# Second group's term rows: four instead of eight transposes each, half of them summed by an accumulating DMA, and two steps moved

## Chip, core and metric

One NeuronCore of a Trainium2 chip runs the whole program. The metric is the device time of one execution in microseconds. A profiled execution has a span (first to last instruction) and a time of its own, which is a little longer than the span.

## What is computed

A block of two parts over 16 sequences of 128 channels by 256 positions. The first part multiplies two projections of a context, convolves the products with a long kernel for each head, and contracts the result with the normalised input; the second is a mixture of eight experts with a capacity, beside a shared feed-forward.

```python
kv = jnp.einsum('bhil,bhjl->bijhl', k_, v_)                  # 8 x 8 products per head, k_ = v_ = ctx
y = irfft(rfft(kv, 2L) * rfft(ssm_kernel, 2L))[..., :L]      # causal convolution of each
out = jnp.einsum('bijhl,bhil->bjhl', y + kv * D, q_)         # q_ = layernorm(x): a sum over i, eight terms
x = x + tanh(g_xattn) * out
x = x + tanh(g_ffn) * moe(layernorm(x))                      # argmax of 8 logits, capacity 256, experts + shared
```

## The kernel before

The 16 sequences are four groups of four (`NG`, `GB`), numbered 0 to 3. The convolution of a group is eight units of two heads; with four groups there are 32 units, one in each **slot** s = 0 to 31 (`CONV` = 32). All engines have the same loop over slots (TensorE at line 1357, DVE at 1124, ACT at 864, POOL at 678), each with its own part of the work, in an order that is written out by hand. The tables `STEPS`, `FIRST_STEPS`, `THIRD_STEPS` and `LAST_STEPS` say how many slots after the end of a group's convolution a step of that group stands; `due(step, s)` turns them into "which group's step is due in slot s". Engines execute in order, and semaphores carry the dependences, so a step that waits holds up everything behind it on its engine.

In a slot s < 32:

- TensorE convolves the unit (`convolve`, lines 1203 and 1206), into one of two places `z`; it must find the products of two units before done (`prods`).
- DVE multiplies the convolution by the queries (`products`, line 509) into `terms`: for each of the unit's two heads eight rows, the eight terms of the sum over i. Six instructions per unit.
- POOL prepares later groups' context products (`kv_products`, lines 490 and 493, every second slot), and for the groups from `FULL_TERMS` = 2 on it adds rows 4 to 7 to rows 0 to 3 of the unit one slot ago (`fold`, line 662).

When a group's eight units are through, TensorE turns `terms` back (`turn_r`, line 1231, two halves k = 0 and 1 in two slots): for each of four 128-column pieces it transposes the rows one after the other into the same place of PSUM, which sums them. `terms_of(g)` is 8 for groups 0 and 1 and 4 for the folded ones: 32 or 16 transposes for each half. DVE adds the result to x (`first_residual`, line 957), and takes the statistics for the second norm (`norm_stats`, lines 923 to 929); POOL makes scale and bias of them (`scale_and_bias`, lines 634 and 635), ACT normalises (`normalise`, line 739), TensorE turns the tokens (`turn_xT`), and ACT and DVE split them into high and low halves (lines 783 and 1070). Router and shared feed-forward follow on TensorE (line 1294), with a silu on ACT (806) and a multiply on DVE (1026) behind each use; the router's logits are copied by ACT (803), turned by TensorE (1255), and DVE chooses the expert (`choose`, lines 974 to 991).

The first norm of a group's queries runs ahead: statistics, scale and apply of group g at slots 8(g-1) + 1, + 2 and + 2, its turn (`turn_q`, line 1218) at 8(g-1) + 5. For group 3 that is 17, 18, 18 and 21. Statistics, scale and apply share single buffers, so the norms go through DVE, POOL and ACT one after another in the order in which their statistics stand.

The places of the change in the code: `FULL_TERMS`, `FIRST_STEPS`, `due`, the fold in POOL's loop (line 683) and the waits of `turn_r` (line 1224). Slots 13 to 21, about 44 to 71 us of the profile, are the stretch in which group 1 is convolved to its end, group 0's tokens go through the router (slots 15 and 16), group 1 is turned (slots 17 and 18) and group 2's convolution has begun (slot 16 on).

Of the kernel before, what the change touches and what calls it, by code (L numbers as in the profile page):

```python
# [32 lines left out]
ALU = mybir.AluOpType  # L33
# [8 lines left out]
NG = 4  # L42
# [17 lines left out]
UNITS = H // 2  # L60
# [11 lines left out]
REST_SLOT = 21  # L72
TERMS = 8
TURNS = 22
FULL_TERMS = 2
HEADS = 24
TROW = HEADS * 64
EXPERT_SPLIT_SLOT = CONV + 12
# [8 lines left out]
    "turn_r0": 1, "turn_r1": 2, "residual0": 2, "residual1": 3, "ln2_stats": 3, "ln2_scale": 4, "ln2_apply": 5,  # L87
    "turn_xT": 6, "tokens_low": 7, "logits": 10, "exp": 10, "places": 12, "gate": 12, "scatter": 12,
}
FIRST_STEPS = {"ln2_stats": 3, "ln2_scale": 3, "ln2_apply": 4, "turn_xT": 5, "tokens_low": 6, "logits": 9, "exp": 9}  # L90
THIRD_STEPS = {"ln2_apply": 4, "logits": 9, "exp": 9, "places": 10, "gate": 10, "scatter": 10}
OWN_STEPS = (FIRST_STEPS, {}, THIRD_STEPS)
LAST_STEPS = {
# [1 line left out]
    "turn_xT": 4, "tokens_low": 5, "logits": 7, "exp": 7, "gate": 8, "places": 9, "scatter": 9,  # L95
}
SCATTER_REST = {24: 0, CONV: 1}
PREPARING = ("ln1_stats", "ln1_scale", "ln1_apply", "turn_q")


def due(step, s):

    if step in PREPARING:
        g, late = divmod(s - STEPS[step], UNITS)
        return g + 1 if late == 0 and 0 < g + 1 < NG else -1
    if s == CONV + LAST_STEPS[step]:
        return NG - 1
    for g, own in enumerate(OWN_STEPS):
        if s == UNITS * (g + 1) + own.get(step, STEPS[step]):
            return g  # L110
    return -1
# [8 lines left out]
def unit(s):  # L120

    g, i = divmod(s, UNITS)
    return g, (i + 4 * (g % 2)) % UNITS
# [97 lines left out]
def build(nc, x, ctxt, kpad, skip_d, g_x, g_f, wg, w1, w3, w2, sw1, sw3, sw2, out):  # L221
# [4 lines left out]
    with ExitStack() as ctx:  # L226
# [3 lines left out]
        def sem(name):  # L230
            return ctx.enter_context(nc.semaphore(name))
# [126 lines left out]
        z_ready = sem("z_ready")  # L358
        prods = sem("prods")
        folded = sem("folded")  # L360
        expert_memory = sem("expert_memory")
        tp_ready = sem("tp_ready")
        tp_free_act = sem("tp_free_act")
# [24 lines left out]
        def view(t, off, dims, parts=P):  # L388

            a = t[:]  # L390
            row = a.ap[0][0]
            return bass.AP(a.tensor, a.offset + off, [[row, parts], *dims])
# [228 lines left out]
        def _(pool):  # L621
# [35 lines left out]
            def fold(s):  # L657
# [3 lines left out]
                             for i in range(2))  # L661
                pool.tensor_tensor(low, low, high, ALU.add).then_inc(folded, 1)  # L662

            def scatter(g, parts):
                for b in parts:
                    n = GB * g + b
                    pool.indirect_dma_start(  # L667
                        out=xd, out_offset=bass.IndirectOffsetOnAxis(ap=dest[:, n:n + 1], axis=0),
                        in_=xrow[:, g % 2, b, :], in_offset=None, bounds_check=E * CAP - 1,
                        oob_is_err=False).then_inc(scattered[g % 2], 16)  # L670
# [7 lines left out]
            for s in range(SLOTS):  # L678
                g, i = kv_due(s)
                if g >= 0:  # L680
                    kv_place_free(pool, g, i)
                    kv_products(pool, g, i, 1, kv_pool)
                if 1 <= s <= CONV and unit(s - 1)[0] >= FULL_TERMS:
                    fold(s - 1)
                for what in ("ln1", "ln2"):
                    if due(what + "_scale", s) >= 0 and (what, due(what + "_scale", s)) != ("ln1", 1):
                        scale_and_bias(NORM_AT[(what, due(what + "_scale", s))])
                if s == SLOTS - 1:
                    pool.wait_ge(z_ready, CONV)
                    pool.memset(bg[:, :, :, :], 0.0).then_inc(pool_consts, 1)  # L690
                g = due("scatter", s)
                if s in SCATTER_REST:
                    scatter(SCATTER_REST[s], range(2, GB))
                if g >= 0:
                    if g == 0:
                        pool.wait_ge(xd_zeroed, 16 * 4)
                    if g >= 2:
                        pool.wait_ge(scattered[g % 2], 16 * GB)
                    pool.iota(xrow[:, g % 2, :, L + 1:L + 2], pattern=[[P, GB], [1, 1]], base=1 + g * GB * P,
                              channel_multiplier=1, allow_small_or_imprecise_dtypes=True).then_inc(numbered, 1)  # L700
                    pool.wait_ge(numbered, g + 1)
                    pool.wait_ge(dest_done, g + 1)
                    pool.wait_ge(gate_done, g + 1)
                    scatter(g, range(2 if g in SCATTER_REST.values() else GB))
                if s == SPLIT_SLOT:
                    split_up()
# [476 lines left out]
        def _(pe):  # L1183
# [37 lines left out]
            def turn_r(g, k):  # L1221
                pe.wait_ge(prods, UNITS * (g + 1))
                if g >= FULL_TERMS:
                    pe.wait_ge(folded, UNITS * (g + 1 - FULL_TERMS))
                n = TP_AT[("r", g, k)]
                tp_wait(pe, n)
                for j in range(2 * BLK):
                    b, blk = 2 * k + j // BLK, j % BLK
                    for t in range(terms_of(g)):
                        src = view(terms, t * TROW + first_head(g, 0) * 64 + blk * GB + b, [[PL, CH]])  # L1230
                        mm = pe.matmul(tp[n % 2][:, j * P:(j + 1) * P], src, ident[:, :], is_transpose=True,  # L1231
                                       start=(t == 0), stop=(t == terms_of(g) - 1))
                mm.then_inc(tp_ready, 1)
# [177 lines left out]
```

## Time and profile before

| | |
|---|---|
| three runs, us | 214.48, 215.14, 214.38; median 214.48 |
| profiled execution, us | 214.29, its span 212.6 |
| mean granted TensorE clock | 0.991 |
| busy in the span | TensorE 198.7 us, DVE 159.9, POOL 123.8, ACT 91.9 |

All times in rows are us from the span's start. A row of the timeline merges equal instructions that follow each other: start, duration until the last of them ends, engine, line, operation, written and read tiles, shape, count, and in brackets how long the engine was idle before and who ended that. Instructions of one engine overlap a little, so the distance from one start to the next is what an instruction takes of its engine.

### The profile page before, as it was taken

Reading aid. Unit: us, or ns where it says so; the run is one execution under the profiler, and the core shown is the slowest. Engines: PE = TensorE matmul, PEld = TensorE weight load, DVE = VectorE, ACT = ScalarE, POOL = GpSimd, SP = SyncE. Lnnn points to the kernel's source line nnn. Section 1 sums busy time; section 2 is a strip of 40 time slices with the busy share of each in tenths; the row PEclk is TensorE's granted clock in tenths of the full one; section 3 lists DMA queues with packets and bytes.
Section 4 is the critical chain, followed back from the end, with each engine's and each line's share of the span. In section 5 each row is a group of like instructions: output and inputs, shape, how many; then the busy total and the mean of one; then the engine's idle time right before and its main releaser. Section 6 shows DMA issues by size and latency. Waiting matters only on the chain.

```text
span 212.6 us, 4239 instructions
## 1 busy us (share of the span) xinstructions
PE 198.7 (93%) x1441; PEld 184.0 (87%) x1441; DVE 159.9 (75%) x518; ACT 91.9 (43%) x182; POOL 123.8 (58%) x129
## 2 busy tenths in 40 slices
PE   5979999899999999999999998999999999999960
PEld 5957789679998989988989998999999999999950
DVE  4798788966998987589867877776856995878530
ACT  2242733193443651322348258654373445624400
POOL 4379999274648599614583253370072687677671
PEclk9999999999999999999999999999999999999996
DMA  5799993000000010010201799845537689422221
GB/s 158 245 339 359 371 396 133 0 0 3 5 0 0 0 53 17 33 54 0 92 10 50 229 357 360 298 125 138 166 106 245 187 261 329 128 78 72 67 91 49
DMA packets 21497, 29.77 MB, mean 140 GB/s; under 512 B 2834, under 2 KB 18970, under 8 KB 21476
## 3 DMA queue, kind: packets, MB, share of 16 engines
q1 hardware_dynamic: 18964, 23.24, 33.3%
q0 software_dynamic: 2304, 6.05, 8.7%
q10 hardware_dynamic: 208, 0.22, 0.4%
q8 instruction: 11, 0.18, 0.4%
q14 instruction: 10, 0.08, 0.1%
HBM read 21.32 MB, written 8.45 MB: 140 GB/s over the span
## 4 chain that ended last, share of the span: by engine, by line
PE 83%; DVE 4%; DMA 4%; issue 3%; ACT 2%; POOLq 1%; ACTq 0%; SPq 0%; DVEq 0%; POOL 0%
PE fb L1294 16%; PE z L1294 14%; PE z L1206 11%; PE tp L1231 10%; PE z L1203 6%; PE z L1315 6%; PE z L1329 5%; PE fb L1329 4%; DMA x_sb<-x 3%; PE fb L1315 2%; DVE terms L509 2%; PE tp L1243 2%; PE tp L1340 2%; DMA dcol<-skip_d 1%; DVE stats L923 1%
## 5 line engine op out<-in xcount | busy, mean ns | idle before, releaser
L509 DVE TENSOR_TENSOR terms<-z,qr 128x512 f32<-128x512 f32 (+2 forms) x192 | 48.9, 326 | 6.5 <-PE z L1206 6.4
L1206 PE MATMUL z<-kv,toep 128*128 128x288 f32 x128 | 41.5, 406 | 0.0
L1294 PE MATMUL fb<-xTh,wh_gu 128*128 128x256 f32 (+1 forms) x104 | 31.9, 306 | 0.2 <-issue 0.2
L490 POOL TENSOR_TENSOR kv<-ct 128x768 f32<-128x768 f32 x15 | 27.4, 1827 | 6.6 <-PE z L1206 3.3
L1203 PEld LDWEIGHTS z<-kv,toep 128*128 128x128 f32 x128 | 22.1, 190 | 9.2 <-issue 4.8
L716 POOL DMA_INDIRECT kv<-out,tok x16 | 20.4, 1273 | 16.3 <-DMA out<-x_sb 11.7
L1203 PE MATMUL z<-kv,toep 128*128 128x144 f32 x128 | 26.8, 291 | 2.8 <-DVE terms L509 1.9
L1294 PE MATMUL fb<-xTl,wh_gu 128*128 128x256 f32 (+1 forms) x104 | 29.0, 279 | 0.0
L1294 PE MATMUL fb<-xTh,wl_gu 128*128 128x256 f32 (+1 forms) x104 | 29.0, 279 | 0.0
L662 POOL TENSOR_TENSOR terms<-terms 128x512 f32<-128x512 f32 x16 | 20.2, 1281 | 14.1 <-DVE terms L509 14.0
L667 POOL DMA_INDIRECT xd_scratch<-xrow,dest x16 | 16.7, 1044 | 17.1 <-DVE xrow L1002 7.3
L1294 PE MATMUL z<-xTh,wh_gu 128*128 128x256 f32 (+1 forms) x88 | 25.3, 287 | 0.0
L1294 PE MATMUL z<-xTl,wh_gu 128*128 128x256 f32 (+1 forms) x88 | 24.5, 278 | 0.0
L1294 PE MATMUL z<-xTh,wl_gu 128*128 128x256 f32 (+1 forms) x88 | 24.4, 277 | 0.0
L727 POOL DMA_INDIRECT out<-kv,tok x16 | 16.1, 1005 | 13.3 <-DVE hL L1026 9.8
L1231 PE MATMUL tp<-ident,terms 128*128 128x128 f32 x192 | 23.0, 277 | 0.0
L1231 PEld LDWEIGHTS tp<-ident,terms 128*128 128x128 f32 x192 | 22.3, 193 | 0.4
L1294 PEld LDWEIGHTS fb<-xTh,wh_gu 128*128 128x128 f32 (+1 forms) x104 | 19.3, 186 | 1.3 <-issue 0.6
L1206 PEld LDWEIGHTS z<-kv,toep 128*128 128x128 f32 x128 | 20.0, 190 | 0.0
L1294 PEld LDWEIGHTS fb<-xTh,wl_gu 128*128 128x128 f32 (+1 forms) x104 | 19.3, 186 | 0.6
L806 ACT ACTIVATE sg<-fb 128x256 f32<-128x256 f32 (+1 forms) x26 | 9.7, 374 | 22.4 <-PE fb L1294 22.3
L1294 PEld LDWEIGHTS fb<-xTl,wh_gu 128*128 128x128 f32 (+1 forms) x104 | 19.2, 185 | 0.0
(154 smaller groups left out, 417.9 us busy)
## 6 DMA issues: line engine op xcount, KB each, us to landing
terms<-w SPq DMA_DIRECT2D x16, 352.0 KB, 4.3
ct<-ctxt SPq DMA_DIRECT2D x3, 768.0 KB, 8.8
xd_scratch<-xrow SPq DMA_DIRECT2D x4, 516.0 KB, 9.7
kv<-xd_scratch SPq DMA_DIRECT2D x8, 258.0 KB, 3.4
out<-x_sb SPq DMA_DIRECT2D x8, 256.0 KB, 2.6
terms<-w SPq DMA_DIRECT2D x8, 256.0 KB, 4.7
x_sb<-x SPq DMA_DIRECT2D x3, 512.0 KB, 6.0
toep<-kskip_scratch SPq DMA_DIRECT2D x3, 512.0 KB, 9.8
```

Of the source, the lines that this page charges most:

```text
L490: eng.tensor_tensor(dst, left, right, ALU.mult)
L509: return eng.tensor_tensor(view(terms, t0 + row * TROW + col, [[64, 2], *td]), view(src, zo, [[512, 2], *zd]), view(qr, q0 + qo, [[CW, 2], ...
L662: pool.tensor_tensor(low, low, high, ALU.add).then_inc(folded, 1)
L667: pool.indirect_dma_start(out=xd, out_offset=bass.IndirectOffsetOnAxis(ap=dest[:, n:n + 1], axis=0), in_=xrow[:, g % 2, b, :], in_offset=N ...
L716: pool.indirect_dma_start(out=bg[:, e % BRING, t, :], out_offset=None, in_=out_rows, in_offset=bass.IndirectOffsetOnAxis(ap=tok[:, e, t:t ...
L727: pool.indirect_dma_start(out=out_rows, out_offset=bass.IndirectOffsetOnAxis(ap=tok[:, e, t:t + 1], axis=0), in_=fin[:, e % 2, t, :], in_o ...
L1203: pe.matmul(view(z[s % 2], k * 512 + GB, [[PL, NPL], [1, GB]]), toep[:, h, P:2 * P], view(kv, o, [[PL, NPL], [1, GB]]), start=True, stop=F ...
L1206: mm = pe.matmul(z[s % 2][:, k, 0:KVH], toep[:, h, 0:P], view(kv, o, [[1, KVH]]), start=False, stop=True, skip_group_check=True)
L1231: mm = pe.matmul(tp[n % 2][:, j * P:(j + 1) * P], src, ident[:, :], is_transpose=True, start=(t == 0), stop=(t == terms_of(g) - 1))
L1294: mm = pe.matmul(bank[0:rows(blk, c), m * 256:(m + 1) * 256], wt[w % 2][:, col:col + rows(blk, c)], xt[:, place, k, first:first + 256], st ...
L1315: mm = pe.matmul(bank[:, t * L:(t + 1) * L], rounded_hidden(blk, c, h_low)[0:rows(blk, c), t * P:(t + 1) * P], rounded_down(blk, d_low, c ...
L1329: mm = pe.matmul(bank[:, t * L:(t + 1) * L], hidden(blk, c)[0:rows(blk, c), t * P:(t + 1) * P], down[0:rows(blk, c), c * L:(c + 1) * L], s ...
```

## The change

Group 1 is folded too: each of its halves is turned with four transposes per piece instead of eight. Of its eight units the first four (slots 8 to 11) are added by one DMA that POOL issues in slot 12: it adds rows 4 to 7 of those eight heads to rows 0 to 3, 128 partitions by 4 rows by 512 numbers, within SBUF. The other four are added by POOL's `fold` in slots 13 to 16, as those of groups 2 and 3 already were in slots 17 to 32. `turn_r` of the groups 1 to 3 waits for the DMA and for a count of additions that now begins with group 1's second half.

The logits of group 0 (and the exponentials behind them) go from slot 17 to 18. The first norm of group 3, that is statistics, scale and apply, goes from slots 17, 18 and 18 to 13, 14 and 14; its turn stays in slot 21.

```diff
-FULL_TERMS = 2
+FULL_TERMS = 1
+SUMMED = 4
...
-FIRST_STEPS = {"ln2_stats": 3, "ln2_scale": 3, "ln2_apply": 4, "turn_xT": 5, "tokens_low": 6, "logits": 9, "exp": 9}
+FIRST_STEPS = {"ln2_stats": 3, "ln2_scale": 3, "ln2_apply": 4, "turn_xT": 5, "tokens_low": 6}
...
+NORM_SOONER = 4
...
     if step in PREPARING:
-        g, late = divmod(s - STEPS[step], UNITS)
-        return g + 1 if late == 0 and 0 < g + 1 < NG else -1
+        sooner = NORM_SOONER if step != "turn_q" else 0
+        return next((g for g in range(1, NG) if s == UNITS * (g - 1) + STEPS[step] - (sooner if g == NG - 1 else 0)), -1)
...
+        summed = sem("summed")
...
+            def sum_rows(g, n):
+                pool.wait_ge(prods, UNITS * g + n)
+                low, high = (view(terms, first_head(g, unit(UNITS * g)[1]) * 64 + i * 4 * TROW,
+                                  [[TROW, 4], [1, 128 * n]]) for i in range(2))
+                pool.dma_start(low, high, accum_op=ALU.add).then_inc(summed, 16)
...
-                if 1 <= s <= CONV and unit(s - 1)[0] >= FULL_TERMS:
+                if s == UNITS + SUMMED:
+                    sum_rows(1, SUMMED)
+                if UNITS + SUMMED < s <= CONV:
                     fold(s - 1)
...
                 if g >= FULL_TERMS:
-                    pe.wait_ge(folded, UNITS * (g + 1 - FULL_TERMS))
+                    pe.wait_ge(summed, 16)
+                    pe.wait_ge(folded, UNITS * g - SUMMED)
```

POOL, from slot 12's context products on, before (`kv` context products, `terms` additions, `rstd` and `nbias` the scale of a norm):

```order
L490 TENSOR_TENSOR kv<-ct 128x4x192
L493 TENSOR_TENSOR kv<-ct 128x4x32
L490 TENSOR_TENSOR kv<-ct 128x4x192
L493 TENSOR_TENSOR kv<-ct 128x4x32
L490 TENSOR_TENSOR kv<-ct 128x4x192
L493 TENSOR_TENSOR kv<-ct 128x4x32
L662 TENSOR_TENSOR terms<-terms 128x4x128
L490 TENSOR_TENSOR kv<-ct 128x4x192
L493 TENSOR_TENSOR kv<-ct 128x4x32
L662 TENSOR_TENSOR terms<-terms 128x4x128
L634 TENSOR_TENSOR rstd<-veps,mhalf 128x4
L635 TENSOR_TENSOR nbias<-mneg,rstd 128x4
```

and now, from the same instruction on (lines of the changed file):

```order
L493 TENSOR_TENSOR kv<-ct 128x4x192
L496 TENSOR_TENSOR kv<-ct 128x4x32
L671 DMA terms<-terms 128x4x512
L665 TENSOR_TENSOR terms<-terms 128x4x128
L493 TENSOR_TENSOR kv<-ct 128x4x192
L496 TENSOR_TENSOR kv<-ct 128x4x32
L665 TENSOR_TENSOR terms<-terms 128x4x128
L637 TENSOR_TENSOR rstd<-veps,mhalf 128x4
L638 TENSOR_TENSOR nbias<-mneg,rstd 128x4
L665 TENSOR_TENSOR terms<-terms 128x4x128
L493 TENSOR_TENSOR kv<-ct 128x4x192
L496 TENSOR_TENSOR kv<-ct 128x4x32
L665 TENSOR_TENSOR terms<-terms 128x4x128 x2
```

The DMA, four additions and group 3's scale have come into the stretch; the last two additions are those of units 15 and 16.

TensorE in slots 17 and 18, before, from the second head's convolution of slot 17 on (`lgT` the logits, `terms` the turns):

```order
L1203 MATMUL z<-kv,toep 128x36x4
L1206 MATMUL z<-kv,toep 128x288
L1255 MATMUL tp<-ident,lgT 128x8 x4
L1231 MATMUL tp<-ident,terms 128x128 x32
L1203 MATMUL z<-kv,toep 128x36x4
L1206 MATMUL z<-kv,toep 128x288
L1203 MATMUL z<-kv,toep 128x36x4
L1206 MATMUL z<-kv,toep 128x288
L1231 MATMUL tp<-ident,terms 128x128 x32
```

and now:

```order
L1214 MATMUL z<-kv,toep 128x36x4
L1217 MATMUL z<-kv,toep 128x288
L1243 MATMUL tp<-ident,terms 128x128 x16
L1214 MATMUL z<-kv,toep 128x36x4
L1217 MATMUL z<-kv,toep 128x288
L1214 MATMUL z<-kv,toep 128x36x4
L1217 MATMUL z<-kv,toep 128x288
L1267 MATMUL tp<-ident,lgT 128x8 x4
L1243 MATMUL tp<-ident,terms 128x128 x16
```

Both turns have half their transposes, and the logits stand between them.

ACT in slots 14 to 17, before (`xTh` and `kv` slot 14, `lgT` and `sg` the router's copy and silu of slots 15 and 16, `xn` the apply of group 3's first norm):

```order
L760 ACTIVATE kv<-ct 128x4x64
L803 ACTIVATE lgT<-fb 8x256
L806 ACT_TABLE_LOAD
L806 ACTIVATE sg<-fb 128x256
L803 ACTIVATE lgT<-fb 8x256
L806 ACTIVATE sg<-fb 128x256
L760 ACTIVATE kv<-ct 128x4x64
L789 ACT_TABLE_LOAD
L789 ACTIVATE ex<-sh 128x32
L760 ACTIVATE kv<-ct 128x4x64
L739 ACTIVATE xn<-x_sb,nbias,rstd 128x256 x4
```

and now:

```order
L771 ACTIVATE kv<-ct 128x4x64
L750 ACTIVATE xn<-x_sb,nbias,rstd 128x256 x4
L814 ACTIVATE lgT<-fb 8x256
L817 ACT_TABLE_LOAD
L817 ACTIVATE sg<-fb 128x256
L814 ACTIVATE lgT<-fb 8x256
L817 ACTIVATE sg<-fb 128x256
L771 ACTIVATE kv<-ct 128x4x64 x2
L800 ACT_TABLE_LOAD
L800 ACTIVATE ex<-sh 128x32
```

The norm stands ahead of slot 15's copy and silu. On DVE the statistics of group 3 stand between the products of slot 13 and the low halves of group 0's tokens (slot 14), and the choice of group 0's experts behind the products of slot 18.

## Rows read from the trace of the kernel before

**Rows 1.** The page's chain that ended last, by engine.

```profile
PE 83%; DVE 4%; DMA 4%; issue 3%; ACT 2%; POOLq 1%; ACTq 0%; SPq 0%; DVEq 0%; POOL 0%
```

**Rows 2.** Table by stretch: window, length, busy us of PE, PEld, DVE, ACT, POOL; clock; DMA.

```profile
40.00:56.00 16.00, 14.66 (x97) 12.49 (x96) 12.48 (x49) 9.68 (x18) 8.83 (x9) 1.00 0.00 2
56.00:72.00 16.00, 16.00 (x122) 14.91 (x121) 14.42 (x64) 5.45 (x12) 11.03 (x13) 1.00 0.00 1
```

**Rows 3.** Timeline of TensorE, slots 15 to 21.

```profile
49.17 0.50 PE L1294 MATMUL fb<-xTh,wh_gu 128*128 128x256 f32 x1
...
55.19 0.41 PE L1255 MATMUL tp<-ident,lgT 8*128 8x8 f32 x4
55.53 3.86 PE L1231 MATMUL tp<-ident,terms 128*128 128x128 f32 x32
59.23 0.41 PE L1203 MATMUL z<-kv,toep 128*128 128x144 f32 x2
...
60.70 3.73 PE L1231 MATMUL tp<-ident,terms 128*128 128x128 f32 x32
64.26 0.41 PE L1203 MATMUL z<-kv,toep 128*128 128x144 f32 x2
...
67.68 0.48 PE L1203 MATMUL z<-kv,toep 128*128 128x144 f32 x2
```

**Rows 4.** Timeline of POOL, slots 12 to 18.

```profile
44.10 0.46 POOL L493 TENSOR_TENSOR kv<-ct 128x128 f32<-128x128 f32 x1
...
56.27 1.82 POOL L490 TENSOR_TENSOR kv<-ct 128x768 f32<-128x768 f32 x1
...
58.47 1.27 POOL L662 TENSOR_TENSOR terms<-terms 128x512 f32<-128x512 f32 x1
59.91 1.02 POOL L634 TENSOR_TENSOR rstd<-veps,mhalf 128x4 f32<-128x4 f32 x1 [0.17 <-DVE mneg L929]
```

**Rows 5.** The page's groups: POOL's DMA issues, count, busy us, mean ns.

```profile
L716 POOL DMA_INDIRECT kv<-out,tok x16 | 20.4, 1273 | 16.3 <-DMA out<-x_sb 11.7
...
L667 POOL DMA_INDIRECT xd_scratch<-xrow,dest x16 | 16.7, 1044 | 17.1 <-DVE xrow L1002 7.3
...
L727 POOL DMA_INDIRECT out<-kv,tok x16 | 16.1, 1005 | 13.3 <-DVE hL L1026 9.8
```

**Rows 6.** The page's DMA rate in 40 slices of 5.3 us; a DMA issue, us to landing.

```profile
GB/s 158 245 339 359 371 396 133 0 0 3 5 0 0 0 53 17 33 54 0 92 10 50 229 357 360 298 125 138 166 106 245 187 261 329 128 78 72 67 91 49
...
terms<-w SPq DMA_DIRECT2D x16, 352.0 KB, 4.3
```

**Rows 7.** Timeline of ACT, slots 15 to 18.

```profile
50.97 0.37 ACT L803 ACTIVATE lgT<-fb 8x256 f32<-8x256 f32 x1 [3.12 <-PE fb L1294]
51.35 1.28 ACT L806 ACT_TABLE_LOAD   x1
52.65 0.39 ACT L806 ACTIVATE sg<-fb 128x256 f32<-128x256 f32 x1
...
61.25 2.08 ACT L739 ACTIVATE xn<-x_sb,nbias,rstd 128x256 f32<-128x256 f32 x4 [0.53 <-POOL nbias L635]
```

**Rows 8.** Timeline of DVE, slots 14 to 18.

```profile
47.09 1.29 DVE L1070 TENSOR_TENSOR xTl<-tp,xTh 128x512 fp32r<-128x512 f32 x2 [1.22 <-ACT xTh L783]
...
53.07 0.42 DVE L1026 TENSOR_TENSOR hL<-fb,sg 128x256 f32<-128x256 f32 x1 [1.78 <-ACT sg L806]
53.41 1.54 DVE L509 TENSOR_TENSOR terms<-z,qr 128x512 f32<-128x512 f32 x6
...
56.76 1.39 DVE L923 BATCH_NORM_STATS2 stats<-x_sb 128x6 f32<-128x256 f32 x4
...
58.60 1.16 DVE L928 TENSOR_SCALAR veps<-mv 128x4 f32<-128x4 f32 x1
...
59.75 0.18 DVE L974 TENSOR_REDUCE mx<-tp 128x4 f32<-128x32 f32 x1
...
61.95 0.75 DVE L957 SCALAR_TENSOR_TENSOR x_sb<-tp,tg,x_sb 128x512 f32<-128x512 f32 x1
```

## The prediction

> **What bounds the kernel now.** I read the chain of waits first: the chain that ended last runs through TensorE for 83% of the span [rows 1]. So I ask where TensorE stands on its own work around the change. The table by stretch says: from 40 to 56 us it is busy 14.66 of 16.00 us, and from 56 to 72 us, where the second group is turned, 16.00 of 16.00, both at a granted clock of 1.00, the 2.4 GHz level [rows 2]; the idle 1.3 us of the first stretch did not lower it, so I price no clock. The timeline of TensorE names the places: slot 17 ends with 32 transposes from 55.53 on, the next convolution begins at 59.23; slot 18 ends with 32 more from 60.70, the next begins at 64.26; slot 21 begins at 67.68 [rows 3]. A transpose taken away there is time off the bound engine, as long as nobody else comes later than TensorE. The timelines of POOL, ACT and DVE then say how late they already are; there the change adds work.
>
> **What it removes.** Each turn has 16 transposes instead of 32. The two runs of 32 last 59.23 - 55.53 = 3.70 and 64.26 - 60.70 = 3.56 us [rows 3]; half of both is 1.85 + 1.78 = 3.63 us. This is the most that the change can give.
>
> **What it adds on POOL.** One accumulating DMA, four additions of 1.27 us [rows 4], and, moved here from slot 18, the scale step: 1.3 us, from its start at 59.91 [rows 4] to ACT's start behind it at 61.25 [rows 7]. Slot 12's products on POOL end at 44.10 + 0.46 = 44.56 [rows 4] and stay where they are. Unknown is how long POOL stands at the DMA's issue. The nearest rows are the indirect DMAs, which POOL issues for 128 rows each: 1273, 1044 and 1005 ns, mean 1.1 [rows 5]. The new one has 128 partitions by 4 rows, 512 pieces: at a price by the piece 4 x 1.1 = 4.4 us, at a price by the instruction 1.1 or somewhat less, since no index is read. I take 1.1, the row itself, and keep 1.0 and 4.4 as ends. The Trainium skill (DMA: Bandwidth & Descriptors, section Anatomy of one DMA — SWDGE (gpsimd) path) calls the generation of descriptors small and says that many can be emitted before their number costs; by it the sum stays as below, by the price per piece it would be the third rival. No row here has both sizes.
>
> POOL's walk from there: issue until 45.65; addition of unit 12 until 46.9; slot 14's products, 2.2 us from 56.27 to the next addition at 58.47 [rows 4], until 49.1; addition of unit 13 until 50.35; scale for the fourth group until **51.65**; addition of unit 14 until 52.95; slot 16's products until 55.15; addition of unit 15 until **56.45**. TensorE needs the last of these for its first turn, ACT the scale for its norm.
>
> **The transfer itself** has from 45.65 to 56.45, 10.8 us. It moves 128 x 4 x 512 x 4 B = 1.05 MB. The DMA engines have nothing else there (0 to 5 GB/s in the slices from 37 to 69 us, but up to 396 in earlier ones) [rows 6]. A weight load of 352 KB lands after 4.3 us [rows 6]; 352 KB at 396 GB/s take 0.9, so 3.4 are fixed. One pass gives 2.65 + 3.4 = 6.0 us; three passes in turn (two read, one written) give 7.95 + 3.4 = 11.3. I take two passes, 8.7 us, hidden with 2 us to spare. Above 10.8 every us is one of TensorE.
>
> **What the sooner norm does on ACT.** ACT issues in order, and the four activations of the norm (2.08 us [rows 7]) now stand in slot 14, ahead of slot 15's silu. They can start at 51.65 and end at 53.75; in the kernel before ACT took that slot's copy at 50.97 [rows 7]. Then copy, table load and silu: 0.3 + 1.28 + 0.39 us [rows 7], until 55.75. DVE's multiply behind that silu ran at 53.07, the products of slot 16 behind it at 53.41 [rows 8]; they go to 55.75 and 56.1, 2.7 us later. So a norm that is used only in slot 21 stands in front of work that TensorE needs at once.
>
> **What it does on DVE.** The statistics of the fourth group move from slot 17 to slot 13. There they took 59.75 - 56.76 = 2.99 us, of which 1.16 is one scalar operation on four numbers per partition at 58.60 [rows 8], beside the POOL addition of 58.47 [rows 4]; and it ends when that addition ends; without it up to 1.1 less, so 1.9 to 3.0 in all. In slot 13 they start at 45.9, where DVE is idle until 47.09 [rows 8], and end at 47.8 to 48.9, so the low halves of the tokens (1.29 us) end at 49.1 to 50.2, and TensorE's router matmuls of slot 15, at 49.17 before [rows 3], come 0 to 1.1 us later. That costs nothing of its own: TensorE would reach the first turn between 55.2 and 56.3, and the last addition ends at 56.45 anyway. In slot 17 DVE is rid of 2.99 us, which nearly cancels ACT's 2.7.
>
> **The sum, along TensorE.** The first turn starts at 56.65 (with 0.2 for the wait) instead of 55.53: 1.1 later. Minus 1.85: it ends at 58.5. Slot 18's convolution (60.70 - 59.23 = 1.47) until 59.95; the logits, moved here, 55.53 - 55.19 = 0.34 [rows 3], until 60.3; the second turn until 62.1, where 64.26 stood: 2.2 ahead. Two convolutions and the places bring TensorE to 65.5 at slot 21, against 67.68. But there it waits for the products of slot 19. DVE: slot 16 from 56.1 until 57.6; multiply 0.35; slot 17 until 59.45; first residual 0.75 until 60.2; slot 18's products until 61.7; choice of the expert, 61.95 - 59.75 = 2.2, until 63.9; second residual until 64.65; slot 19's products 1.54 until 66.2 [rows 8]. TensorE goes on at about 66.3: **1.4 us ahead**. So 2.2 of the 3.6 are given back: 1.1 in front of the first turn, 0.3 for the logits that now stand between the turns, 0.8 behind the second. All that follows hangs on TensorE or on semaphores that move with it, so I carry 1.4 to the end. The logits' later slot costs nothing: DVE comes to them at 61.7, long after 60.3; the places that need the choice come at 65. The group's x is loaded long before (the bus is idle from 37 us [rows 6]). SP's queue is not touched.
>
> Against the profiled execution's own 214.29 us this gives 212.9. The median of the runs is 0.19 higher, so **213.1** is the forecast.
>
> **Rivals.** 0.5% (1.07 us) is about what a measurement of this kernel can tell from no change.
>
> First, TensorE keeps more: if DVE's share is shorter than walked, slot 21 starts when TensorE gets there, at 65.5, and the gain is 2.2: 212.3. For it: the additions and the norm may come a little sooner. Against it: every duration on DVE has a row. Chance 0.07.
>
> Second, a dearer issue, 1.45 to 3.5 us. Each us more at the issue moves the scale, ACT's silu, the products of slot 16 and the last addition by one us, so the gain is 1.4 - (issue - 1.1): zero at 2.5. Say 214.0, inside 0.5%. For it: 512 pieces are four times the nearest row's. Chance 0.24.
>
> Third, on the other side: **the price by the piece, ACT stuck behind the norm.** Place: POOL's issue at 44.56, then ACT in slot 14. Price: at 4.4 us all walks shift by 3.3, that is 1.9 us slower, 216.4. It decides from 2.5 us of issue on, and beyond 3.6 us it is slower by more than 0.5%. Against it: the indirect rows read an index and compare it with a bound for every piece, which this DMA does not. Chance 0.11.
>
> Fourth, the transfer lands late: an adding DMA reads both operands and writes one, and the 11.3 us of three passes is no hard ceiling, as no row shows one. It costs nothing until 10.8 us after the issue, has eaten the gain at 12.2, and is slower by over 0.5% from 13.3; at 14 us 216.2. The Trainium skill (Collectives: The Full Stack, section The bandwidth ceiling: the fold count and why AG ≠ RS ≠ AR) says that the adding itself costs no cycles and the second read halves the rate; by it the transfer is the two passes above and stays hidden. Chance 0.16: 0.06 within 0.5%, 0.10 slower.
>
> **How the numbers follow.** The forecast has 0.42. Faster by over 0.5%: 0.42 + 0.07 = 0.49. Within: 0.24 + 0.06 = 0.30. Slower: 0.11 + 0.10 = 0.21. The range runs from 212.0 (the first rival less the runs' spread) to 215.8 (an issue of 3.8 us, or a landing at 13.6); beyond it I leave some 0.15. The likeliest case alone, with an issue of 1.0 to 1.4 us, is 212.9 to 213.4.
>
> **What would show it.** In the profile after: a DMA on POOL at 44.5 of about 1.1 us; 160 transposes at the turns' line, where 192 stood; ACT's four norm activations starting at 51.6 and DVE's products of slot 16 at 56.1; TensorE's first turn at 56.6 waiting for POOL's last addition, not for the DMA; a wait of 0.8 us for DVE ahead of slot 21. Wrong it would be by a POOL issue above 1.5 us, a first turn that ends its wait on the DMA, or a norm that ACT can start before 50 us.

## The result and the profile after

The changed kernel takes 219.37 us (six runs, 218.84 to 219.93) against 214.41 us (214.22 to 215.14) of the kernel before on the same chip: ratio 1.0231 [1.0211, 1.0250], **5 us slower**, where 1.3 us faster was forecast. Ratios here compare fast executions: those over 1.5% above the fastest of the same kernel are left out, which happens in e7 alone, its profiled one included. The profiled execution took 218.84 us, its span is 217.1 us. Nearly all is lost between slots 15 and 22. The first convolutions of these two slots, before and after:

```profile
47.93 0.41 PE L1203 MATMUL z<-kv,toep 128*128 128x144 f32 x2
71.70 0.41 PE L1203 MATMUL z<-kv,toep 128*128 128x144 f32 x2
...
47.12 0.41 PE L1214 MATMUL z<-kv,toep 128*128 128x144 f32 x2
75.35 0.41 PE L1214 MATMUL z<-kv,toep 128*128 128x144 f32 x2
```

That is 23.77 us before and 28.23 after, 4.46 more; from there to slot 31 the two traces run in parallel (3.65 us apart at slot 22, 3.79 at slot 31). The lead of 0.81 us at slot 15 is older than the change's stretch: at slot 1 it is 0.76 already, where TensorE before waited 0.90 us for a DMA. Behind slot 31 the changed trace loses about as much.

The chain of waits of the changed kernel, by engine, which answers to [rows 1]: TensorE has lost 12 points of it, VectorE has won 6.

```profile
PE 71%; DVE 10%; issue 7%; DMA 3%; ACT 3%; POOL 3%; POOLq 1%; ACTq 0%; DVEq 0%
```

The table by stretch of the changed kernel, columns as in [rows 2], first the same two stretches, then the end of the second one cut finer:

```profile
40.00:56.00 16.00, 12.12 (x80) 10.16 (x79) 14.11 (x46) 9.13 (x18) 14.04 (x14) 1.00 0.39 67
56.00:72.00 16.00, 12.60 (x80) 10.66 (x79) 14.17 (x50) 4.52 (x8) 11.18 (x11) 0.95 0.00 1
...
68.00:69.80 1.80, 0.00 (x0) 0.00 (x0) 1.76 (x8) 0.00 (x0) 0.00 (x0) 1.00 0.00 0
69.80:72.00 2.20, 2.11 (x8) 1.74 (x9) 2.13 (x11) 0.00 (x0) 1.45 (x2) 0.63 0.00 0
72.00:74.00 2.00, 2.00 (x11) 1.86 (x9) 1.90 (x12) 0.00 (x0) 1.15 (x3) 0.55 0.00 0
```

TensorE is idle for 3.9 us of the first stretch and 3.4 of the second, GpSimd works 14.0 us of the first instead of 8.8, and behind the idle stretch before 69.8 us the granted clock is at 0.63 and 0.55, near 0.5, the 1.2 GHz level.

TensorE's timeline in the changed kernel, slots 15 to 21 (before: [rows 3]):

```profile
51.30 0.39 PE L1306 MATMUL fb<-xTh,wh_gu 128*128 128x256 f32 x1 [2.55 <-DVE xTl L1081]
...
57.77 2.03 PE L1243 MATMUL tp<-ident,terms 128*128 128x128 f32 x16 [0.40 <-POOL terms L665]
...
61.54 2.06 PE L1243 MATMUL tp<-ident,terms 128*128 128x128 f32 x16
...
69.89 0.48 PE L1214 MATMUL z<-kv,toep 128*128 128x144 f32 x2 [3.00 <-DVE terms L512]
```

The turns are halved as forecast. The two long waits that did not exist before, 2.55 us at the router of slot 15 and 3.00 us at slot 21, both end on VectorE. Its timeline (before: [rows 8]):

```profile
44.99 1.39 DVE L934 BATCH_NORM_STATS2 stats<-x_sb 128x6 f32<-128x256 f32 x4
...
46.83 3.15 DVE L939 TENSOR_SCALAR veps<-mv 128x4 f32<-128x4 f32 x1
...
49.97 1.27 DVE L1081 TENSOR_TENSOR xTl<-tp,xTh 128x512 fp32r<-128x512 f32 x2
...
59.85 0.75 DVE L968 SCALAR_TENSOR_TENSOR x_sb<-tp,tg,x_sb 128x512 f32<-128x512 f32 x1 [0.64 <-PE tp L1243]
...
62.83 0.18 DVE L985 TENSOR_REDUCE mx<-tp 128x4 f32<-128x32 f32 x1
63.04 0.19 DVE L986 TENSOR_TENSOR sh<-tp,mx 128x32 f32<-128x32 f32 x1
63.27 1.04 DVE L988 SCALAR_TENSOR_TENSOR t<-sh,prio 128x32 f32<-128x32 f32 x1
...
65.34 1.72 DVE L1000 TENSOR_TENSOR acc<-acc,oh 128x8 f32<-128x8 f32 x1
...
67.19 0.19 DVE L1002 TENSOR_REDUCE mine<-t 128x4 f32<-128x32 f32 x1
67.41 0.75 DVE L968 SCALAR_TENSOR_TENSOR x_sb<-tp,tg,x_sb 128x512 f32<-128x512 f32 x1
```

And GpSimd's (before: [rows 4]):

```profile
43.70 1.54 POOL L671 DMA_DIRECT2D terms<-terms  x1
44.76 1.81 POOL L665 TENSOR_TENSOR terms<-terms 128x512 f32<-128x512 f32 x1
46.00 2.33 POOL L493 TENSOR_TENSOR kv<-ct 128x768 f32<-128x768 f32 x1
47.77 0.96 POOL L496 TENSOR_TENSOR kv<-ct 128x128 f32<-128x128 f32 x1
48.18 1.76 POOL L665 TENSOR_TENSOR terms<-terms 128x512 f32<-128x512 f32 x1
50.13 1.03 POOL L637 TENSOR_TENSOR rstd<-veps,mhalf 128x4 f32<-128x4 f32 x1 [0.19 <-DVE mneg L940]
...
62.99 1.27 POOL L665 TENSOR_TENSOR terms<-terms 128x512 f32<-128x512 f32 x1 [0.78 <-DVE terms L512]
65.21 1.82 POOL L493 TENSOR_TENSOR kv<-ct 128x768 f32<-128x768 f32 x1 [0.95 <-PE z L1217]
66.99 0.48 POOL L496 TENSOR_TENSOR kv<-ct 128x128 f32<-128x128 f32 x1
```

Read the two together. Line 939 adds a constant to four numbers per partition. It starts at 46.83 and ends at 49.98, just after GpSimd's addition of 48.18 ends (49.94). Line 988 ends at 64.31, GpSimd's addition at 64.26; line 1000 ends at 67.06, GpSimd's product at 67.03. Where GpSimd rests beside them, the three take 0.17 to 0.19 us (e4 and e6 below). Beside the same addition of 62.99, line 986 (an operand in PSUM) takes 0.19, and beside the product of 66.99 line 1002 (a reduction) takes 0.19. So those that wait are a scalar operation and instructions with two inputs in SBUF, and what they wait for is GpSimd. Not all of GpSimd's work holds them: in the kernel before, line 977 (988 here) ran inside GpSimd's scale step of 59.91 to 60.93 [rows 4] and did not wait:

```profile
60.19 0.19 DVE L977 SCALAR_TENSOR_TENSOR t<-sh,prio 128x32 f32<-128x32 f32 x1
```

The choice of expert takes 67.41 - 62.83 = **4.58 us** instead of 2.2, the statistics 49.97 - 44.99 = **4.98 us** instead of 3.0.

The Trainium skill (SBUF — State Buffer, section Who interferes with whom) says that VectorE and GpSimd share one pair of SBUF ports as an exclusive lock, held for a whole instruction, which a scalar operation in its two-port mode or a VectorE instruction with two SBUF inputs needs, and a reduction does not. The trace agrees on which instructions wait, but for line 977 above; that line 939 runs in that mode no trace here shows. It differs on how long: if the lock passes on at the end of one instruction of the other engine, the wait at line 939 is some 1 us (to 47.77, where GpSimd's next one starts); the trace has 3.15, over three.

Theory from these rows: the change fills GpSimd in slots 12 to 18, and its moves put VectorE's small SBUF instructions beside that. Rivals: the norm's apply, which now stands ahead of slot 15's silu on ScalarE; the accumulating DMA itself; the moves by themselves.

### The profile page after: what moved, and what is told of

It reads as the page before. It is cut to its first block, busy times and chain, and to the rows that moved or that the text cites. A ratio compares the mean times of both kernels' runs of the same rounds, so it can differ in the third digit from the quotient of the medians.

```text
span 217.1 us, 4186 instructions
## 1 busy us (share of the span) xinstructions
PE 196.7 (91%) x1409; PEld 180.9 (83%) x1409; DVE 163.1 (75%) x518; ACT 91.8 (42%) x182; POOL 129.6 (60%) x134
## 4 chain that ended last, share of the span: by engine, by line
PE 71%; DVE 10%; issue 7%; DMA 3%; ACT 3%; POOL 3%; POOLq 1%; ACTq 0%; DVEq 0%
PE fb L1306 15%; PE z L1306 13%; PE z L1217 9%; PE tp L1243 8%; PE z L1327 6%; PE z L1214 5%; DVE terms L512 4%; PE z L1341 4%; PE fb L1341 4%; DMA ct<-ctxt 3%; PE fb L1327 2%; PE tp L1352 2%; DVE stats L934 2%; POOL terms L665 1%; PE tp L1255 1%
## 5 line engine op out<-in xcount | busy, mean ns | idle before, releaser
L1217 PE MATMUL z<-kv,toep 128*128 128x288 f32 x128 | 42.4, 413 | 0.0
L665 POOL TENSOR_TENSOR terms<-terms 128x512 f32<-128x512 f32 x20 | 26.5, 1337 | 13.9 <-DVE terms L512 13.9
L1214 PEld LDWEIGHTS z<-kv,toep 128*128 128x128 f32 x128 | 22.4, 192 | 11.4 <-issue 6.6
L493 POOL TENSOR_TENSOR kv<-ct 128x768 f32<-128x768 f32 x15 | 27.9, 1862 | 4.8 <-DMA ct<-ctxt 3.8
L1217 PEld LDWEIGHTS z<-kv,toep 128*128 128x128 f32 x128 | 20.3, 192 | 0.0
L1243 PE MATMUL tp<-ident,terms 128*128 128x128 f32 x160 | 19.4, 278 | 0.4 <-POOL terms L665 0.4
L1243 PEld LDWEIGHTS tp<-ident,terms 128*128 128x128 f32 x160 | 18.6, 193 | 1.1 <-DVE terms L512 0.8
```

The source lines that it names most:

```text
L493: eng.tensor_tensor(dst, left, right, ALU.mult)
L1214: pe.matmul(view(z[s % 2], k * 512 + GB, [[PL, NPL], [1, GB]]), toep[:, h, P:2 * P], view(kv, o, [[PL, NPL], [1, GB]]), start=True, stop=F ...
L1217: mm = pe.matmul(z[s % 2][:, k, 0:KVH], toep[:, h, 0:P], view(kv, o, [[1, KVH]]), start=False, stop=True, skip_group_check=True)
```

## The experiments

The table holds every run against the kernel before on the same chip, and, out of TensorE's timeline, the time from slot 15's first convolution to slot 22's, less the 23.77 us before, and its wait ahead of slot 21. Of e7 only the times are used.

| run | ratio to before | slots 15 to 22, us | wait at slot 21, us |
|---|---|---|---|
| the change | 1.0231 [1.0211, 1.0250] | +4.46 | 3.00 |
| e1, norm back | 1.0169 [1.0137, 1.0201] | +3.40 | 2.54 |
| e2, logits back | 1.0071 [1.0043, 1.0099] | +1.55 | 0.17, and 1.16 at slot 20 |
| e3, sums alone | 0.9999 [0.9984, 1.0014] | -0.13 | 0.18, and 0.40 at slot 20 |
| e4, moves alone | 0.9994 [0.9975, 1.0013] | 0.01 | none |
| e5, scale first | 1.0239 [1.0204, 1.0273] | +3.33 | 2.99 |
| e6, choice held clear | 1.0096 [1.0064, 1.0129] | +1.65 | 0.61 |
| e7, e5 and e6 | 1.0023 [0.9990, 1.0057] | | |
| e8, no DMA | 1.0234 [1.0201, 1.0267] | +2.59, and 3.15 behind at slot 15 | 3.01 |
| e9, e7 and additions first | 0.9939 [0.9920, 0.9959] | -1.09 | 1.62 |
| e10, e9 and choice later | 0.9940 [0.9921, 0.9959] | -2.08 | none, and 1.03 for ScalarE behind it |
| e11, e10 and all additions first | 0.9948 [0.9932, 0.9965] | -2.06 | none, and 1.03 for ScalarE behind it |

### Which part of the change costs (e1 to e4)

e1 takes the sooner norm back:

```diff
-NORM_SOONER = 4
+NORM_SOONER = 0
```

> The change with the fourth group's first norm left where it was (statistics in slot 17); the sums by the DMA and the later logits stay. Theory (the small VectorE instructions whose operands all lie in SBUF wait until GpSimd's row of instructions ends, and the choice of expert in slot 18 is the wait that counts): slot 16 starts where it did before (the 3.15 us at L939 in slot 13 are gone), but the statistics, 1.9 us and their own wait for GpSimd, now stand among the products of slots 17 to 19, so the wait of TensorE at slot 21 (3.00 us) is as long or longer: 218 to 221 us. Rival (the sooner norm on ScalarE, ahead of slot 15's silu, is the cause): 213 to 215 us. Rival (the accumulating DMA's own traffic slows the engines): 218 to 220 us, with VectorE's instructions of slots 13 to 16 still long.

217.76 us. Every range is missed, the theory's by 0.2 us; the direction is the theory's. Slot 16 is back in its place, but the statistics of slot 17 and the choice of slot 18 now both wait (1.47 us at the scalar operation, 1.04 and 1.79 in the choice), and TensorE waits 2.54 us at slot 21. The norm on ScalarE is not the main cause: without it 3.6 us of the loss (1.7%) stay.

e2 takes the logits back:

```diff
+FIRST_STEPS = {"ln2_stats": 3, "ln2_scale": 3, "ln2_apply": 4, "turn_xT": 5, "tokens_low": 6, "logits": 9, "exp": 9}
```

> The change with the first group's logits and exponentials left in the slot before (17); the sums by the DMA and the sooner norm stay. Theory: the choice of expert now comes right behind the products of slot 17, while GpSimd adds and multiplies without a pause from 56.2 to 62.2 us, so it takes 4 us or more there too instead of 2.2, and it holds the first residual, so TensorE's wait comes at slot 19 or 20 and is 2 to 4 us: 217 to 221 us. Rival (the later logits themselves cost the time, whatever GpSimd does): the choice takes 2.2 us and the time is 214 to 215.5 us.

215.97 us, between the two ranges. The choice takes 4.02 us (59.38 to 63.40), with 1.05 and 1.14 at two instructions, so it waits there too; but TensorE meets it in two short waits, and slot 21 to slot 22 takes 4.59 us against 5.46 in the change.

e3 has both edits. e4 is the changed kernel without the sums:

```diff
-FULL_TERMS = 1
-SUMMED = 4
+FULL_TERMS = 2
...
-if s == UNITS + SUMMED:
-    sum_rows(1, SUMMED)
-if UNITS + SUMMED < s <= CONV:
+if 1 <= s <= CONV and unit(s - 1)[0] >= FULL_TERMS:
     fold(s - 1)
...
-pe.wait_ge(summed, 16)
-pe.wait_ge(folded, UNITS * g - SUMMED)
+pe.wait_ge(folded, UNITS * (g + 1 - FULL_TERMS))
```

> Both moves undone: only the summing of the second group's rows to four, half by the DMA, is left. Theory: slots 13 to 16 as before but for GpSimd; the statistics and the choice stand in slot 17, where GpSimd is now at work without a pause, and each waits for it; VectorE is behind from slot 18 on: 215.5 to 220 us. Rival (the two moves are what costs): below 214 us. Rival (the DMA's traffic): additions and products that run beside the transfer (8.6 us from its issue) are over 10% longer.

> The kernel before with both moves and without the sums: group 1 keeps 64 turning matrix products, no DMA and no additions of GpSimd for that group. Theory: in slot 13 GpSimd has only one product pair (1.8 and 0.5 us), so L939's counterpart ends by 48.3 us (at most 1.8 us instead of 3.15); the choice in slot 18 meets the additions of the third group as in the change, but TensorE has 3.6 us more of its own work to cover it: 213.5 to 215.5 us. Rival (the moves alone cost, the sums are free): 217 to 219.5 us.

214.25 and 214.04 us: **each half alone changes nothing**, together they cost 2.3%. e4 is inside the theory's range. e3 came out below it, and just above the first rival's 214; of the second rival's sign it has the longer records of GpSimd (1.82 us for the first addition behind the DMA's issue), but they go on to 59 us, where the transfer landed at 52.3 (43.91 + 8.4), and the starts lie no further apart. The sums alone gain on TensorE what was forecast, and lose it to VectorE. In e3 the convolution of slot 18 is 1.7 us ahead, set against slot 15; from there on VectorE works without a pause and TensorE waits for it four times, the longest wait being this one, for the choice, ahead of the second turn:

```profile
60.28 2.03 PE L1243 MATMUL tp<-ident,terms 128*128 128x128 f32 x16 [1.68 <-DVE t L988]
```

In e4 GpSimd has no additions for the second group, and VectorE's statistics run free; the choice still waits once, but TensorE has its own 3.6 us to cover it:

```profile
46.97 0.17 DVE L928 TENSOR_SCALAR veps<-mv 128x4 f32<-128x4 f32 x1
...
61.65 1.04 DVE L977 SCALAR_TENSOR_TENSOR t<-sh,prio 128x32 f32<-128x32 f32 x1
```

### Which wait, and is it GpSimd (e5 to e8)

e5 and e6 leave VectorE's instructions as they are and only keep GpSimd off them, by order or by one semaphore:

```diff
 for s in range(SLOTS):                                   # GpSimd
+    if s == 2 * UNITS + 3:                               # e6, e7
+        pool.wait_ge(picked, 1)
+    if due("ln1_scale", s) == NG - 1:                    # e5, e7; not again below
+        scale_and_bias(NORM_AT[("ln1", NG - 1)])
     g, i = kv_due(s)
...
-    chain(dve.tensor_reduce(mine[:, :], t3[:, :, :], AX_X, ALU.add))
+    dve.tensor_reduce(mine[:, :], t3[:, :, :], AX_X, ALU.add).then_inc(picked, 1)
+    dve.wait_ge(picked, g + 1)
```

e8 drops the DMA; GpSimd adds all eight units of the second group:

```diff
-SUMMED = 4
+SUMMED = 0
...
-if s == UNITS + SUMMED:
-    sum_rows(1, SUMMED)
...
-pe.wait_ge(summed, 16)
```

> The change, with GpSimd's scale of the fourth group's first norm ahead of its multiplication and its addition in slot 14, instead of behind them; nothing else. GpSimd then waits for the statistics with nothing of its own running. Theory (VectorE's small SBUF instructions wait until GpSimd's row of instructions ends): L939 takes 0.2 us instead of 3.15, slot 16 starts some 2.9 us sooner than in the change, as in the kernel before; the choice in slot 18 still waits for GpSimd, and as TensorE comes sooner, its wait at slot 21 is 2 to 4 us as before: 215.5 to 218 us. Rival (the 3.15 us come of the DMA, not of GpSimd's instructions): L939 stays over 2 us and the time within 0.5% of the change's 219.4 us.

> The change, with GpSimd made to wait, ahead of its work of slot 19, until the choice of expert of slot 18 is done (a semaphore on the choice's last instruction); nothing else. Theory: the choice takes 2.2 to 2.4 us instead of 4.6, TensorE's wait at slot 21 falls from 3.0 to some 0.5 us, with it the low clock of 70 to 74 us goes: 215 to 216.5 us, though L939 in slot 13 still takes 3.1 us. Rival (GpSimd's held work is late in its turn, and the wait moves): 218 us or more, with a wait of TensorE or of ScalarE for GpSimd later. Rival (the wait in slot 13 is the one that counts): within 0.5% of 219.4 us.

> Both: GpSimd's scale first in slot 14, and GpSimd waiting in slot 19 until the choice is done. Theory: both waits are gone, VectorE's row from slot 16 to slot 20 is 1.5 us ahead of that of the sums alone, and the change's own idea is seen without GpSimd in the way: 212 to 213.7 us, faster than the kernel before (214.2 us). Rival (VectorE's own work fills slots 16 to 21 with or without these waits): 214 to 215 us.

> The change without its DMA: all eight units of the second group are added by GpSimd (four more additions of 1.3 us in slots 9 to 12, one instead of the issue of 1.1 us). Theory: L939 still waits for GpSimd, to the end of one instruction or of the row of them (1 to 3.2 us), and the choice still takes over 4 us: 217 to 220 us. Rival (the transfer of 1 MB between 45 and 53 us, or something that the issue does to GpSimd's later instructions, whose records overlap by 0.5 us behind it, is the cause): L939 is under 1 us, and the time 214 to 216 us.

e6, 216.98 us, is the clearest. The same choice with GpSimd held, in VectorE's and TensorE's timelines of e6:

```profile
64.30 0.19 DVE L991 SCALAR_TENSOR_TENSOR t<-sh,prio 128x32 f32<-128x32 f32 x1
...
65.52 0.17 DVE L1003 TENSOR_TENSOR acc<-acc,oh 128x8 f32<-128x8 f32 x1
```

```profile
68.53 0.48 PE L1218 MATMUL z<-kv,toep 128*128 128x144 f32 x2 [0.61 <-DVE terms L513]
```

The choice takes 2.20 us, TensorE's wait falls from 3.00 to 0.61 us as forecast, and the clock stays up there:

```profile
69.80:72.00 2.20, 2.20 (x18) 1.97 (x16) 2.17 (x10) 0.32 (x1) 2.00 (x2) 1.00 0.00 0
```

Slot 21 to slot 22 takes 4.44 us instead of 5.46, so the low clock cost some 1.0 us. The time is 0.5 us above the expected range: from slot 15 to 22, 1.65 us are still lost, to the statistics in slot 13, which here too took 3.16 us. In this trace the wait that they cause at the router is as long as in the change, but here the clock falls behind it, to the 1.2 GHz level:

```profile
51.73 0.58 PE L1310 MATMUL fb<-xTh,wh_gu 128*128 128x256 f32 x1 [2.56 <-DVE xTl L1085]
```

```profile
52.00:54.00 2.00, 2.00 (x10) 2.00 (x11) 2.00 (x9) 1.99 (x4) 0.79 (x1) 0.50 0.02 5
```

The router's twelve products, to the start of slot 16 at 54.46 us, take 2.73 us, against 1.54 in the change (51.30 to 52.84).

e5 clears those, and line 941, its counterpart of 939, takes 0.17 us; slot 16 starts on time. But the time stays: 219.96 us, ratio 1.0239, outside the expected 215.5 to 218. GpSimd's row, with the scale in front, still ends the last addition that the first turn needs only at 57.09 us; TensorE is there 2.36 us sooner, and waits. From TensorE's timeline of e5:

```profile
57.34 2.03 PE L1245 MATMUL tp<-ident,terms 128*128 128x128 f32 x16 [2.36 <-POOL terms L665]
```

Its profile is 1.1 us better than the change's up to slot 22; the timed runs do not bear that out, and the profiled execution is the fastest of its four. e7, both together, missed its 212 to 213.7 us, and the rival's 214 to 215: median 216.21 us, runs from 213.69 to 217.84, ratio 1.0023.

e8, 220.26 us, 0.3 above the theory's range, clears the DMA of the loss at slot 21: the choice takes 4.59 us (63.81 to 68.40), TensorE's wait 3.01. The long wait needs no DMA either. In slot 9, where GpSimd now adds as well, the statistics of the third group's first norm on VectorE, and GpSimd beside them:

```profile
33.44 2.76 DVE L937 TENSOR_SCALAR veps<-mv 128x4 f32<-128x4 f32 x1
```

```profile
32.72 1.81 POOL L493 TENSOR_TENSOR kv<-ct 128x768 f32<-128x768 f32 x1
34.49 0.44 POOL L496 TENSOR_TENSOR kv<-ct 128x128 f32<-128x128 f32 x1
34.91 1.26 POOL L665 TENSOR_TENSOR terms<-terms 128x512 f32<-128x512 f32 x1
```

VectorE waits out all three (to 36.17), in a program without that DMA; in the change the same operation takes 0.37 us (at 32.68). In slot 13 of e8 it is otherwise:

```profile
49.77 1.03 DVE L937 TENSOR_SCALAR veps<-mv 128x4 f32<-128x4 f32 x1
50.71 0.50 DVE L938 TENSOR_SCALAR mneg<-mv 128x4 f32<-128x4 f32 x1
```

```profile
48.95 1.82 POOL L493 TENSOR_TENSOR kv<-ct 128x768 f32<-128x768 f32 x1
50.74 0.45 POOL L496 TENSOR_TENSOR kv<-ct 128x128 f32<-128x128 f32 x1
```

Here each VectorE instruction waits for **one** GpSimd instruction (to 50.80, then to 51.21) and slips in between. Behind the DMA's issue, in the change, GpSimd's instructions start as far apart as ever (1.24, 1.77 and 0.41 us) but their records are 0.5 us longer and overlap the next one by that; there VectorE found no gap in three instructions, but at 33.44 in e8 it found none either, with overlaps of 0.04 us at most. What decides between one instruction and three stays open. The wait in slot 9 is also where e8's own loss ahead of slot 14 begins: the products of slots 11 and 12 start at 42.87 us, 2.0 us later than in the change, set against slot 9; TensorE waits 2.75 us for them at 44.55 us (0.93 in the change, at 41.79), and the clock is at 0.58 from 46 to 50 us.

### A version that keeps the idea (e9 to e11)

e9 is e7 with GpSimd's additions of slots 13 to 16 ahead of its products of the same slot, which TensorE needs only eight slots later:

```diff
+    if UNITS + SUMMED < s <= 2 * UNITS:
+        fold(s - 1)
     g, i = kv_due(s)
...
-    if UNITS + SUMMED < s <= CONV:
+    if 2 * UNITS < s <= CONV:
         fold(s - 1)
```

e10 moves the choice of e9 to slot 19, with its places, gates and scatter in slot 21, and holds GpSimd in slot 20, behind the scale of that slot; e11 puts the additions of e10 first in every slot:

```diff
+FIRST_STEPS = {"ln2_stats": 3, "ln2_scale": 3, "ln2_apply": 4, "turn_xT": 5, "tokens_low": 6, "logits": 11, "exp": 11, "places": 13, "gate": 13, "scatter": 13}
...
-    if s == 2 * UNITS + 3:
-        pool.wait_ge(picked, 1)
+    if s == 2 * UNITS + 4:
+        scale_and_bias(NORM_AT[("ln2", 1)])
+        pool.wait_ge(picked, 1)
-    if UNITS + SUMMED < s <= 2 * UNITS:                  # e11
+    if UNITS + SUMMED < s <= CONV:                       # e11
         fold(s - 1)
...
```

> Both waits cleared (GpSimd's scale first in slot 14, GpSimd waiting in slot 19 until the choice is done), and GpSimd's additions of slots 13 to 16 put ahead of its multiplications of the same slot. In the run with both cleared the scale first pushed the last addition to 57.4 us, TensorE waited 2.36 us for it, and the turning products then took 3.48 us for 16 instead of 2.03. Theory (what is left of the loss there is this wait alone): the last addition ends by 54 us, the first turning follows slot 17 without a wait, slot 18 starts near 57.2 us instead of 61.0, and most of that is kept through slot 22: 211.5 to 213.5 us, ratio to the kernel before 0.985 to 0.997. Rival (VectorE's own instructions fill slots 16 to 22, as they do with the sums alone, which stood at 1.00): ratio 0.997 to 1.003, with TensorE's waits for VectorE at slots 20 to 22 adding up to over 1.5 us.

> The same, with the first group's choice moved once more, to slot 19 behind the second group's statistics (its places, gates and scatter one slot later too), and GpSimd held in slot 20 until it is done. Theory (the choice is the one step of VectorE there that nothing of TensorE's next two slots needs): TensorE's wait at slot 21 is gone, 0.5 to 1 us faster than the run with the additions first. Rival (VectorE has no slack up to slot 24): within 0.3% of that run, the wait standing at slot 22 or 23 instead.

> The run with the choice one slot later again, with GpSimd's additions ahead of its multiplications in all later slots too (up to slot 32) and not only in slots 13 to 16. In that run TensorE was 3.3 us ahead of the kernel before up to slot 25, and lost 1.2 us there in a wait of 0.99 us for GpSimd's last addition of the third group, which stood behind a multiplication of 2.2 us and two scatters. Theory (that wait alone lost it): the wait goes, slot 26 is 3 us ahead, and the ratio to the kernel before falls to 0.986 to 0.992. Rival (the lead is lost further on, in a wait for a later step): ratio 0.992 to 0.996, as without.

e9 beats both kernels: 213.53 us against 214.65 of the kernel before on its chip, ratio 0.9939 [0.9920, 0.9959]. It differs from e7 in the order of the additions alone. TensorE and VectorE of e9:

```profile
55.37 2.03 PE L1251 MATMUL tp<-ident,terms 128*128 128x128 f32 x16 [0.19 <-DVE terms L513]
...
66.08 0.48 PE L1222 MATMUL z<-kv,toep 128*128 128x144 f32 x2 [1.62 <-DVE terms L513]
```

```profile
60.86 1.19 DVE L995 SCALAR_TENSOR_TENSOR t<-sh,prio 128x32 f32<-128x32 f32 x1
```

The first turn follows at once, and slot 21 starts at 66.08 us (slot 15 was 0.09 us earlier than before), where the prediction has 66.3. The theory's ratio holds, but so does the rival's wait: 1.62 us for VectorE, 1.0 of it one instruction of the choice that met the addition of slot 18, ahead of the hold.

e10 and e11 fell short of what I expected: e10 is as fast as e9, which is its rival's range, though with the wait elsewhere, and e11's ratio is in its rival's range. Both are 2.1 us ahead at slot 22, set against slot 15, with no wait at slot 21; but both lose 1.2 us in slot 25, where TensorE waits for GpSimd's last addition of the third group. It stands at 82.57 us in e10 and at 83.04 us in e11, with the same length:

```profile
83.04 2.02 PE L1250 MATMUL tp<-ident,terms 128*128 128x128 f32 x16 [0.99 <-POOL terms L666]
```

In e11 the additions went ahead of the products and the wait did not move, so the products were not its cause; in both, GpSimd is idle until 73.9 and 74.4 us, waiting for the gate weights that now come later, then has its scatters to issue. That the scatters are the cause was not tried. The three versions are equal within their intervals.

## Why the prediction was wrong, point by point

- **TensorE's saving, 3.63 us.** Right: the turns take 59.64 - 57.77 = 1.87 us and 63.44 - 61.54 = 1.90, together 3.49 us less than before.
- **The DMA.** Right, and with it the second, third and fourth rivals fall. GpSimd goes on 44.76 - 43.70 = 1.06 us after its issue (1.1 forecast), the transfer lands after 8.6 us (8.7), and nobody waits for it: the first turn waited for GpSimd's addition. From the list of DMA issues, size and us to landing:

```profile
terms<-terms POOLq DMA_DIRECT2D x1, 1024.0 KB, 8.6
```

- **ScalarE behind the sooner norm.** The order is right: the silu's copy follows the norm at 53.46 us without a pause. The numbers (51.6 and 56.1 us forecast, 51.47 and 55.89 measured) are right in part by luck: this trace is 0.81 us ahead at slot 15, so both come some 0.6 us later than forecast. It is not on the path: behind it VectorE still waits 0.64 us, at 59.85, for the first turn. In e9, where GpSimd's scale stands first, the norm starts at 49.21 us and the products of slot 16 at 53.62 (53.41 before).
- **The statistics in slot 13, "1.9 to 3.0 in all", which "costs nothing of its own".** This step failed. I had seen that the 1.16 us of line 928 [rows 8] end with one addition of GpSimd, and took that one addition as the bound. My own walk of GpSimd had the additions and products of slots 13 and 14 there without a pause. They took 4.98 us, the products of slots 14 and 15 came later, with them the last additions, and the first turn started at 57.77 us instead of 56.65, in a trace that was 0.8 us earlier at slot 15. None of the four rivals had this wait or the next one, and 219.37 us lies beyond the 215.8 at which the range ends.
- **The choice of expert, "61.95 - 59.75 = 2.2".** This step failed and cost the most. The duration came from a place where GpSimd made its scale, 1.2 us of small instructions [rows 4]; it was carried to slot 18, where additions and products of 0.5 to 1.8 us stand. It measured 4.58 us, all on the path to slot 21.
- **"So I price no clock."** This step failed behind the other two: after an idle time of 3.00 us, which I did not forecast, the clock was at 0.63 and 0.55. Slot 21's convolutions and the router behind them took 4.59 us (69.89 to 74.48), against 2.96 in e6 (68.53 to 71.49); some 1.0 us of that reached slot 22.
- **The sum.** Forecast 1.4 us ahead, measured 4.46 behind at slot 22: 5.9 us apart. Keeping GpSimd off the choice gives 2.8 of it back (e6), keeping it off the statistics and its additions in time 2.7 more (e9). That lands on the forecast within 0.4 us, but in part by luck: in e9 the first turn starts at 55.37 us, 1.3 us sooner than forecast, and the choice takes 3.19 us (60.42 to 63.61) instead of 2.2. No run has the forecast's program with VectorE never waiting for GpSimd.

## What to carry to other kernels

A duration holds where its neighbours are the same. Before you move a small VectorE instruction that works on SBUF alone, see what GpSimd does in the place it goes to, and take GpSimd's unbroken row of additions and products there as the upper bound of its cost. Two edits that are each free can cost together when one fills an engine and the other moves work beside it: price the second in the program that the first leaves. Order and one semaphore on the engine with slack kept them apart here but for 1.0 us (e9).

## What the runs showed of the hardware

- In the thirteen traces 47 VectorE instructions of the statistics, the choices and the places take over 0.3 us (nearly all others 0.15 to 0.19), and each ends 0.02 to 0.05 us behind the end of an addition or a product of GpSimd.
- Such an instruction waited out one GpSimd instruction in slot 13 of e8 (1.03 and 0.50 us), and three in a row in the change (3.15 us, behind an accumulating DMA's issue) and in slot 9 of e8 (2.76 us, without that DMA). Why one or three is open. Inside GpSimd's scale step of 128x4 numbers one took 0.19 us (60.19 in the kernel before): it did not wait.
- An accumulating DMA of 1 MB within SBUF held GpSimd for 1.06 us and landed after 8.6 us. Behind its issue GpSimd's records are 0.5 us longer and overlap, in e1 and e3 until GpSimd's next pause, 14 us and more later. Why is open.
- Idle time alone does not say whether TensorE's clock falls: it was at 0.63 and 0.55 behind the 3.00 us at slot 21. With 2.55 us at the router it was at 1.00 over the whole stretch from 40 to 56 us in the change, and with 2.56 us in the same place at 0.50 from 52 to 54 us in e6.
